# TensorE's order of work by strips of an adjacency matrix: runs of four chunks, one accumulator bank, and the feature store on ACT's queue

## The chip, the cores and the metric

The kernel runs on one core of a Trainium2 chip. The core has engines that work side by side: TensorE (PE in the profile; PEld are its weight loads), VectorE (DVE), ScalarE (ACT), GpSimd (POOL) and SyncE (SP, which here only issues DMA). Each executes its own instructions in order and they meet through semaphores. The metric is the device time of one launch in microseconds; lower is better.

## The reference, cut to what matters

A layer of a graph network on 8192 nodes with 64 features, with a dense 8192 x 8192 float32 adjacency matrix A (268 MB), and a graph attention layer behind it:

```python
h = relu(layernorm(x))                                   # 8192 x 64
hid = tanh(concat([h, t]) @ W1 + b1)
XB = h @ B.T
x = x + hid @ W2 + b2 + A @ XB - A.sum(axis=1, keepdims=True) * XB
h = relu(layernorm(x))
feats = (h @ W).reshape(-1, 8, 8)
scores = leaky_relu(a_self(feats)[i] + a_neigh(feats)[j], 0.2) + (-1e10 * (1 - A))
x = x + relu(softmax(scores, over j) @ feats + bias)
```

The mask is scaled by 1e10, so with these inputs only the largest entry of a row keeps weight in the softmax: the kernel finds the column of each row's largest entry while it reads A once, and fetches the features of that node. A general path for other data stands behind a flag and isn't run with these inputs.

## The kernel before

**Tiling.** A is read once, laid out as 16 strips of 512 rows (`S`), each as 8 chunks (`NC`) of 2 MB: a chunk is 128 partitions by 8 blocks of 512 float32. Chunks go through a ring of four slots in SBUF (`ring`, `RING` 4). SP issues the load of chunk c into its slot when TensorE has counted the old chunk in that slot as done (`pe_chunk`) and so has DVE (`hi_done`), lines 264 to 268.

**TensorE** does two things with each chunk. `products(c)` (L726): 8 matmuls of 128 x 64 weights (h of the nodes) by 512 columns, added into a bank `acc`, two side by side in halves of the bank. `sums(c)` (L734): 8 matmuls of a 128 x 32 block of ones by the same columns into the bank `row_sums`, four side by side. The profile counts two instructions for each of these float32 matmuls, so that one chunk is a row x16 and two chunks x32. A function `chunk` alternates the order so that like stands by like: even chunks products first, odd chunks sums first. A strip in this order is P0 S0 | turns | S1 P1 P2 S2 S3 P3 P4 S4 | turn of h1 | S5 P5 | features, hidden | P6 S6 S7 P7, and P7 stands beside P0 of the next strip. `acc` has two banks, one for even, one for odd strips.

**The small work of a strip** belongs to the strip before: `turn_maxima(s-1)` and `turn_sums(s-1)` (L782, L768 to L775) bring row maxima, sums and products of strip s-1 to node order, `turn_h1(s-1)` (L789) turns the normalised features, `features(s-1)` (L796) multiplies them by the attention layer's weights, and `mlp_hidden(s)` (L754) computes the input of tanh for strip s.

**ACT**, per strip and in this order (`finish_strip(s)`, then `tanh(s+1)`): copy of `acc` (L421) and of `row_sums` (L422) when all 8 chunks are done, copy of the turned sums (L424), the strip of h for the next hidden layer (L415), a square root for the layernorm (L428, with a table load of its own), relu of the turned h1 (L431), copy of the features to SBUF (L433), and the tanh of the next strip (L409, also with a table load). TensorE waits for the copy of the row sums (`rows_copied`) before the first sums of the next strip overwrite their bank; these stand behind the products of chunk 0 (L747). `turn_sums` waits for both copies and for the tanh.

**DVE** folds each chunk into running maxima of 128 x 2048 (L508 to L514), folds these further at the strip's end (L520 to L525), then searches the maxima's places and does the layernorm of strip s-1 between the chunks of strip s. **POOL** fetches candidates, and after the last strip the features of each node's partner, 64 gathers (L367). **SP** stores the features of strip s-1 to DRAM (L275) behind the loads of strip s; it first waits for ACT's copy (`feat_done`), and the loads of the next strip are queued behind that wait.

The loops: ACT and TensorE go over pairs of strips, since the bank alternates; DVE and SP over single ones.

Of the kernel before, what the change touches and what calls it, by code (L numbers as in the profile page):

```python
# [29 lines left out]
D = 64  # L30
# [3 lines left out]
W = 512  # L34
S = N // W
# [16 lines left out]
def build(nc, x, adj, adj_t, w1, w1_t, b1, t_in, w2, b2, b_t, w_gat, w_gat_t, att_self, att_neigh, bias, out):  # L52
    with ExitStack() as ctx:
# [98 lines left out]
        pro_h = sem("pro_h")  # L152
        chunk_in = [sem(f"chunk_in{r}") for r in range(RING)]
        pe_chunk = sem("pe_chunk")
        lo_done = sem("lo_done")
        hi_done = sem("hi_done")
        fold = sem("fold")
# [81 lines left out]
        @block.sync  # L239
        def _(sp):  # L240
            for k, (b0, b1_) in enumerate(((0, 2 * CB), (2 * CB, NB))):
                sp.dma_start(x_pb[:, b0:b1_, :], x_by_p[:, b0:b1_, :]).then_inc(x_in[k], 16)
            for n in range(RING):
                sp.dma_start(slot(n), adj_t[n]).then_inc(chunk_in[n % RING], 16)
            sp.dma_start(x_tq[:, :, :].rearrange("q (s k) d -> q s (k d)", k=TB), x_by_q).then_inc(x_tq_in, 16)

            def load_weights():
                for dst, src in ((w_gat_t_sb[:, :], w_gat_t), (w1_sb[0:D, 0:HID], w1), (w1_sb[D:P, HID:2 * HID], w1), (w2_sb[:, :], w2),
                                 (hid_bias[:, 0:1], b1), (hid_bias[:, 1:2], w1_t),
                                 (hid_bias[:, 2:3], t_in.to_broadcast([HID, 1])),  # L250
                                 (b_t_twice[0:D, :], b_t), (b_t_twice[D:P, :], b_t),
                                 (b_t_diag[0:D, 0:D], b_t), (b_t_diag[D:P, D:2 * D], b_t),
                                 (b2_row[:, :], b2.to_broadcast([P, D])),
                                 (w_ext[0:D, 0:D], w_gat), (w_ext[D:P, FA:FA + D], w_gat), (bias_row[:, :], bias.to_broadcast([P, D]))):
                    sp.dma_start(dst, src).then_inc(consts_in, 16)  # L255
                sp.dma_start(att_col[:, 0:1], att_self).then_inc(att_in, 16)
                sp.dma_start(att_col[:, 1:2], att_neigh).then_inc(att_in, 16)

            sp.wait_ge(pool_const, 12)
            load_weights()  # L260

            def load(s, c):

                sp.wait_ge(pe_chunk, s * NC + (c - RING + 1))
                sp.wait_ge(hi_done, s * NC + (c - RING + 1))
                sp.sem_inc(sp_past, 1)
                src = adj_t[bass.ds(s * NC + c, 1)].rearrange("a p f -> (a p) f")
                sp.dma_start(slot(c), src).then_inc(chunk_in[c % RING], 16)

            def store_feats(s):  # L270

                sp.wait_ge(feat_done, s + 1)
                sp.sem_inc(sp_past, 1)
                dst = feats_by_q[:, bass.ds(s, 1), :].rearrange("q a (k d) -> q (a k) d", d=D)
                sp.dma_start(dst, feats_v[:, bass.ds(s * TB, TB), 0:D]).then_inc(feat_stored, 16)  # L275

            for c in range(RING, NC):
                load(0, c)
            with sp.Fori(1, S) as s:
                for c in range(NC):  # L280
                    load(s, c)
                store_feats(s - 1)
            store_feats(S - 1)
            for g in range(QG):
                sp.wait_ge(out_done, g + 1)
                ts = slice(g * OG, (g + 1) * OG)
                sp.dma_start(out_by_q[:, g * OG // TB:(g + 1) * OG // TB, :],
                             gathered[:, ts, :].rearrange("q (s k) d -> q s (k d)", k=TB)).then_inc(stored, 16)
            sp.wait_ge(stored, 16 * QG)

            sp.wait_ge(flag_done, 1)
            general = sp.value_load(flag[0:1, 0:1], min_val=0, max_val=1)
            with sp.If(general != 0):
                sp.wait_ge(gen_copied, NB // 4)
                sp.dma_start(neigh_dram, h_t[0:HEADS, :]).then_inc(gen_neigh_stored, 16)
                sp.wait_ge(gen_neigh_stored, 16)
                adj_rows = adj.rearrange("(s q k) j -> s k q j", q=P, k=TB)
                out_rows = out.rearrange("(s q k) d -> s k q d", q=P, k=TB)
                with sp.Fori(0, S) as s:
                    for k in range(TB):  # L300
                        ib = s * TB + k
                        sp.wait_ge(gen_head, s * (TB * HEADS) + (k * HEADS + 1))
                        sp.sem_inc(sp_past, 1)
                        sp.dma_start(ring[:, 0:N], adj_rows[bass.ds(s, 1), k].rearrange("a q j -> (a q) j"))\
                            .then_inc(gen_row_in, 16)
                        with sp.Fori(0, HEADS) as h:
                            sp.wait_ge(gen_head, ib * HEADS + h + 1)
                            sp.sem_inc(sp_past, 1)
                            sp.dma_start(ring[:, N:2 * N], neigh_dram[bass.ds(h, 1), :].to_broadcast([P, N]))\
                                .then_inc(gen_neigh_in, 16)  # L310
                        sp.wait_ge(gen_out, s * TB + (k + 1))
                        sp.sem_inc(sp_past, 1)
                        sp.dma_start(out_rows[bass.ds(s, 1), k].rearrange("a q d -> (a q) d"), tmp[:, 0, :])\
                            .then_inc(gen_stored, 16)
                        sp.wait_ge(gen_stored, s * (16 * TB) + (k * 16 + 16))
                        sp.sem_inc(sp_past, 1)
# [57 lines left out]
        def _(act):  # L374
# [40 lines left out]
                    act.copy(h_strip[k * D:(k + 1) * D, :].rearrange("d (m q) -> d m q", q=P),  # L415
                             h_by_k[:, 2 * k:2 * k + 2, bass.ds(s * P, P)]).then_inc(strip_h_done, 1)

            def finish_strip(s, parity, last=False):

                act.wait_ge(pe_chunk, s * NC + NC)  # L420
                act.copy(acc_sb[:, :], acc[parity][:, :]).then_inc(acc_copied, 1)  # L421
                act.copy(row_sb[:, :], row_sums[:, :]).then_inc(rows_copied, 1)  # L422
                act.wait_ge(acc_turned, s + 1)
                act.copy(acc_tq[:, :, :], ps_acc[:, :, 0:D + 1]).then_inc(acc_tq_done, 1)  # L424
                if not last:
# [6 lines left out]
                act.wait_ge(feat_ready, s + 1)  # L432
                act.copy(feats[:, bass.ds(s * (TB * FA), TB * FA)],  # L433
                         ps_feat[:, :, :].rearrange("q t f -> q (t f)")).then_inc(feat_done, 1)

            act.wait_ge(pro_h, 2 * NC)
            strip_h(0)
            act.wait_ge(dve_const, 4)
            tanh(0)
            with act.Fori(0, S // 2 - 1) as r:  # L440
                for k in range(2):
                    finish_strip(2 * r + k, k)
                    tanh(2 * r + k + 1)
            finish_strip(S - 2, 0)
            tanh(S - 1)
            finish_strip(S - 1, 1, last=True)

            act.wait_ge(flag_done, 1)
            general = act.value_load(flag[0:1, 0:1], min_val=0, max_val=1)
# [260 lines left out]
        def _(pe):  # L710
# [6 lines left out]
                    last = pe.transpose(pro_banks[k // 4][:, k % 4, :], x_pb[:, g * CB + k, :], ident[:, :])  # L717
                last.then_inc(pro_turned, 1)

            def products(s, c, parity):  # L720


                pe.wait_ge(chunk_in[c % RING], s * (16 * NC // RING) + 16 * (c // RING + 1))
                for b in range(CB):
                    at = (b % 2) * D
                    last = pe.matmul(acc[parity][at:at + D, :], x_pb[:, c * CB + b, :], slot(c)[:, b * W:(b + 1) * W],  # L726
                                     start=(c == 0 and b < 2), stop=(c == NC - 1 and b >= CB - 2))
                return last

            def sums(c):  # L730
# [3 lines left out]
                    last = pe.matmul(row_sums[at:at + QUAD, :], ones_cols[:, :], slot(c)[:, b * W:(b + 1) * W],  # L734
                                     start=(c == 0 and b < 4), stop=(c == NC - 1 and b >= CB - 4))
                return last

            def chunk(s, c, parity, first=False):


                if c % 2:
                    pe.wait_ge(chunk_in[c % RING], s * (16 * NC // RING) + 16 * (c // RING + 1))
                    sums(c)
                last = products(s, c, parity)
                if c % 2 == 0:
                    if c == 0 and not first:
                        pe.wait_ge(rows_copied, s)  # L747
                    last = sums(c)
                last.then_inc(pe_chunk, 1)

            def mlp_hidden(s):
                pe.wait_ge(strip_h_done, 2 * s + 2)
# [44 lines left out]
                                     h1_t[:, m * P:(m + 1) * P], w_ext[:, :], start=True, stop=True)  # L797
                last.then_inc(feat_ready, 1)

            def strip(s, parity):  # L800

                for c in range(NC):
                    if c == 1:
                        turn_maxima(s - 1)
                        turn_sums(s - 1)
                    chunk(s, c, parity)
                    if c == 4:
                        turn_h1(s - 1, ps_turn)
                    if c == 5:
                        features(s - 1)  # L810
                        mlp_hidden(s)

            for c in range(NC):
                pe.wait_ge(pro_norm, c + 1)
                chunk(0, c, 0, first=True)
                if c == 0:
                    pe.wait_ge(pool_const, 12)
                turn_first(c)
# [6 lines left out]
            pe.wait_ge(dve_const, 6)  # L825
            pe.wait_ge(w_ext_done, 2)
            mlp_hidden(0)
            with pe.Fori(0, S // 2 - 1) as r:
                strip(2 * r + 1, 1)
                strip(2 * r + 2, 0)  # L830
            strip(S - 1, 1)
            turn_maxima(S - 1)
            turn_sums(S - 1)
            turn_h1(S - 1, ps_hid)
# [76 lines left out]
```

## Time and profile before

| | |
|---|---|
| time, median of 3 runs | 904.38 us (903.35 to 905.34) |
| profiled execution, its own time | 904.73 us |
| its span, first to last instruction | 903.5 us |
| mean granted TensorE clock | 0.941 |
| busy: PE, DVE, POOL, ACT | 776.9, 729.3, 173.4, 128.5 us |
| HBM read | 277.10 MB |

All times in the profile are microseconds unless marked ns. A row of the grouped view names line, engine and operation, what is written from what, shapes, count, then busy time, the mean of one, and the idle time ahead with what ended it. In a timeline the first two numbers are the start of a group, from the start of the span, and its length; x is the count, and brackets hold the idle time before it. Matmuls are pipelined, and a group's length includes the tail of its last one, so the start of the next group is the better edge. A granted clock of 1.00 is 2.4 GHz and 0.50 is 1.2 GHz.

The span has three stages: to about 80 us the first strip, together with the layernorm of x; to about 800 us fifteen strips; and the rest, the gathers on POOL, in which TensorE has almost no work.

### The profile page before, as it was taken

The numbers are of one execution on the slowest core, as the hardware profiler recorded it, in microseconds if no ns is written. First come the engines' busy times: TensorE is split into PE (matmuls) and PEld (weight loads), VectorE is DVE, ScalarE is ACT, GpSimd is POOL, SyncE is SP. The second block draws the span as 40 slices with busy tenths as digits, with TensorE's granted clock in tenths as the row PEclk, the third lists the DMA queues.
The fourth block names the chain that finished last, engine by engine and source line by source line (L and its number), as shares of the span: only waits on it lengthen the run. The fifth ranks groups of instructions, "written<-read, shape, count | busy, mean of one in ns | idle before, by whom it ended". The sixth has DMA issues, their size and how long they took to land.

```text
span 903.5 us, 13331 instructions
## 1 busy us (share of the span) xinstructions
PE 776.9 (86%) x5222; PEld 266.7 (30%) x5222; DVE 729.3 (81%) x958; ACT 128.5 (14%) x212; POOL 173.4 (19%) x160
## 2 busy tenths in 40 slices
PE   3898999999999999999999999999999999940000
PEld 1333232333333333333332323233333333320000
DVE  5889968989898989898989898998989897952111
ACT  2424011111111111111010201111111111110000
POOL 1000302020110202020202020202011020217774
PEclk9999999999999999999999999999999999985555
DMA  9797879697979797979798897979797979502221
GB/s 375 280 428 288 321 291 422 271 424 288 425 288 426 284 429 280 429 291 418 319 390 364 345 410 300 420 290 422 289 421 287 425 283 429 214 11 40 60 49 41
DMA packets 37267, 281.58 MB, mean 312 GB/s; under 512 B 14336, under 2 KB 18560, under 8 KB 20736
## 3 DMA queue, kind: packets, MB, share of 16 engines
q1 hardware_dynamic: 33152, 277.12, 74.9%
q0 software_dynamic: 4096, 4.20, 2.0%
q8 instruction: 13, 0.21, 0.1%
q14 instruction: 6, 0.05, 0.0%
HBM read 277.10 MB, written 4.19 MB: 311 GB/s over the span
## 4 chain that ended last, share of the span: by engine, by line
PE 74%; POOL 7%; DVE 5%; issue 4%; DMA 4%; SPq 4%; ACT 0%; POOLq 0%; DVEq 0%
PE acc L726 44%; PE row_sums L734 22%; POOL gathered L367 7%; DMA ring<-in_adj_t 4%; SPq L255 4%; DVE max_hi L514 2%; PE ps_hid L754 2%; PE ps_feat L796 1%; PE ps_xb L775 1%; PE ps_acc L768 1%; PE ps_turn L782 1%; PE ps_acc L771 1%; PE ps_acc L773 1%; PE ps_turn L789 1%; DVE max_lo L513 0%
## 5 line engine op out<-in xcount | busy, mean ns | idle before, releaser
L726 PE MATMUL acc<-ring,x_pb 128*64 128x512 f32 x2048 | 462.8, 601 | 18.4 <-DMA ring<-in_adj_t 18.4
L513 DVE TENSOR_TENSOR max_lo<-max_lo,ring 128x2048 f32<-128x2048 f32 x96 | 220.6, 2298 | 44.7 <-DMA ring<-in_adj_t 44.2
L734 PE MATMUL row_sums<-ring,ones_cols 128*32 128x512 f32 x2048 | 240.0, 597 | 0.0
L726 PEld LDWEIGHTS acc<-ring,x_pb 128*64 128x64 f32 x2048 | 141.0, 138 | 326.1 <-issue 326.1
L514 DVE TENSOR_TENSOR max_hi<-max_hi,ring 128x2048 f32<-128x2048 f32 x96 | 219.7, 2289 | 0.0
L358 POOL DMA_INDIRECT cand<-in_adj,cls_row x64 | 78.0, 1218 | 663.5 <-DVE cls_row L543 648.9
L734 PEld LDWEIGHTS row_sums<-ring,ones_cols 128*32 128x32 f32 x2048 | 56.5, 109 | 151.6 <-issue 149.8
L367 POOL DMA_INDIRECT gathered<-feats_dram,best x64 | 62.8, 981 | 19.5 <-issue 19.5
L651 DVE TENSOR_TENSOR gathered<-gathered,bias_row 128x512 f32<-128x512 f32 x8 | 5.6, 703 | 67.5 <-DMA gathered<-feats_dram,best 67.5
L508 DVE TENSOR_TENSOR max_lo<-ring 128x2048 f32<-128x2048 f32 x16 | 36.7, 2292 | 4.4 <-DMA ring<-in_adj_t 2.5
L510 DVE TENSOR_TENSOR max_hi<-ring 128x2048 f32<-128x2048 f32 x16 | 36.6, 2288 | 4.2 <-DMA ring<-in_adj_t 3.9
L520 DVE TENSOR_TENSOR max_lo<-max_lo,max_hi 128x2048 f32<-128x2048 f32 x16 | 36.7, 2292 | 2.0
L349 POOL TENSOR_TENSOR x_tq<-x_tq,b_row 128x256 f32 x16 | 30.2, 1888 | 37.0 <-DMA bias_row<-in_bias 36.8
L428 ACT ACTIVATE stat<-stat,eps 128x4 f32<-128x4 f32 x16 | 4.8, 298 | 196.0 <-DVE stat L585 196.0
L421 ACT COPY acc_sb<-acc 128x512 f32<-128x512 f32 x16 | 9.4, 586 | 136.6 <-PE acc L726 136.6
L424 ACT COPY acc_tq<-ps_acc 128x260 f32<-128x260 f32 x16 | 6.0, 376 | 106.7 <-PE ps_xb L775 106.7
L409 ACT ACT_TABLE_LOAD x16 | 20.5, 1283 | 2.5 <-PE ps_hid L754 2.3
L428 ACT ACT_TABLE_LOAD x16 | 20.5, 1283 | 0.3
L522 DVE TENSOR_TENSOR max_lo<-max_lo 128x1024 f32<-128x1024 f32 x16 | 19.6, 1225 | 0.5
L754 PE MATMUL ps_hid<-h_strip,w_sb 128*128 128x256 f32 x64 | 17.4, 397 | 3.0 <-ACT h_strip L415 3.0
L433 ACT COPY feats<-ps_feat 128x320 f32 (+1 forms) x16 | 6.8, 426 | 89.6 <-PE ps_feat L796 89.6
L431 ACT ACTIVATE h_t<-ps_turn 128x256 f32<-128x256 f32 x15 | 5.8, 386 | 93.2 <-PE ps_turn L789 93.2
(95 smaller groups left out, 423.3 us busy)
## 6 DMA issues: line engine op xcount, KB each, us to landing
ring<-in_adj_t SPq DMA_DIRECT2D x128, 2048.0 KB, 11.3
x_tq<-in_x SPq DMA_DIRECT2D x1, 2048.0 KB, 30.8
feats_dram<-feats SPq DMA_DIRECT2D x16, 128.0 KB, 2.3
out<-gathered SPq DMA_DIRECT2D x8, 256.0 KB
x_pb<-in_x SPq DMA_DIRECT2D x1, 1536.0 KB, 7.8
cand<-in_adj,cls_row POOLq DMA_INDIRECT x64
gathered<-feats_dram,best POOLq DMA_INDIRECT x64
x_pb<-in_x SPq DMA_DIRECT2D x1, 512.0 KB, 4.6
```

The lines of the kernel that those rows point to most:

```text
L255: sp.dma_start(dst, src).then_inc(consts_in, 16)
L349: pool.tensor_tensor(x1, x1, b2_row[:, :].unsqueeze(1).to_broadcast([P, TB, D]), ALU.add).then_inc(x_b2_done, 1)
L358: pool.indirect_dma_start(out=cand[:, k, :], out_offset=None, in_=classes, in_offset=bass.IndirectOffsetOnAxis(ap=cls_row[:, k:k + 1], axi ...
L367: pool.indirect_dma_start(out=gathered[:, t, :], out_offset=None, in_=feats_dram, in_offset=bass.IndirectOffsetOnAxis(ap=best[:, t:t + 1], ...
L508: dve.tensor_tensor(max_lo[:, :], lo, hi, ALU.max).then_inc(hi_done, 1)
L510: dve.tensor_tensor(max_hi[:, :], lo, hi, ALU.max).then_inc(hi_done, 1)
L513: dve.tensor_tensor(max_lo[:, :], max_lo[:, :], lo, ALU.max).then_inc(lo_done, 1)
L514: dve.tensor_tensor(max_hi[:, :], max_hi[:, :], hi, ALU.max).then_inc(hi_done, 1)
L520: dve.tensor_tensor(max_lo[:, :], max_lo[:, :], max_hi[:, :], ALU.max).then_inc(fold, 1)
L726: last = pe.matmul(acc[parity][at:at + D, :], x_pb[:, c * CB + b, :], slot(c)[:, b * W:(b + 1) * W], start=(c == 0 and b < 2), stop=(c == ...
L734: last = pe.matmul(row_sums[at:at + QUAD, :], ones_cols[:, :], slot(c)[:, b * W:(b + 1) * W], start=(c == 0 and b < 4), stop=(c == NC - 1 ...
L754: last = pe.matmul(ps_hid[:, k * (W // 2):(k + 1) * (W // 2)], w1_sb[:, k * HID:(k + 1) * HID], h_strip[:, :], start=True, stop=True)
```

## The change

TensorE's strip is written out. Its order is S0 S1 | turns | P0 P1 P2 P3 S2 S3 S4 S5 | turn of h1 | P4 P5 P6 P7 S6 S7 | features, hidden, and S0 S1 of the next strip follow. The wait for `rows_copied` stands at the head of the strip. One bank `acc[0]` serves all strips, a new semaphore `acc_full` counts the end of P7, and ACT waits for that before it copies `acc`. Chunks are counted as done behind P0, P1, S2, S3, P4, P5, S6, S7. In the first strip sums stand before products but for chunk 7. ACT issues the store of the features itself, right after its copy of them and a wait for it; SP's stores and their waits are gone. The loops go over single strips.

```diff
         pe_chunk = sem("pe_chunk")
+        acc_full = sem("acc_full")
...
                 src = adj_t[bass.ds(s * NC + c, 1)].rearrange("a p f -> (a p) f")
                 sp.dma_start(slot(c), src).then_inc(chunk_in[c % RING], 16)
 
-            def store_feats(s):
-
-                sp.wait_ge(feat_done, s + 1)
-                sp.sem_inc(sp_past, 1)
-                dst = feats_by_q[:, bass.ds(s, 1), :].rearrange("q a (k d) -> q (a k) d", d=D)
-                sp.dma_start(dst, feats_v[:, bass.ds(s * TB, TB), 0:D]).then_inc(feat_stored, 16)
-
             for c in range(RING, NC):
                 load(0, c)
             with sp.Fori(1, S) as s:
                 for c in range(NC):
                     load(s, c)
-                store_feats(s - 1)
-            store_feats(S - 1)
...
-            def finish_strip(s, parity, last=False):
-
+            def finish_strip(s, last=False):
+
+                act.wait_ge(acc_full, s + 1)
+                act.copy(acc_sb[:, :], acc[0][:, :]).then_inc(acc_copied, 1)
                 act.wait_ge(pe_chunk, s * NC + NC)
-                act.copy(acc_sb[:, :], acc[parity][:, :]).then_inc(acc_copied, 1)
                 act.copy(row_sb[:, :], row_sums[:, :]).then_inc(rows_copied, 1)
                 act.wait_ge(acc_turned, s + 1)
                 act.copy(acc_tq[:, :, :], ps_acc[:, :, 0:D + 1]).then_inc(acc_tq_done, 1)
                 act.wait_ge(feat_ready, s + 1)
                 act.copy(feats[:, bass.ds(s * (TB * FA), TB * FA)],
                          ps_feat[:, :, :].rearrange("q t f -> q (t f)")).then_inc(feat_done, 1)
+                act.wait_ge(feat_done, s + 1)
+                dst = feats_by_q[:, bass.ds(s, 1), :].rearrange("q a (k d) -> q (a k) d", d=D)
+                act.dma_start(dst, feats_v[:, bass.ds(s * TB, TB), 0:D]).then_inc(feat_stored, 16)
 
             tanh(0)
-            with act.Fori(0, S // 2 - 1) as r:
-                for k in range(2):
-                    finish_strip(2 * r + k, k)
-                    tanh(2 * r + k + 1)
-            finish_strip(S - 2, 0)
-            tanh(S - 1)
-            finish_strip(S - 1, 1, last=True)
+            with act.Fori(0, S - 1) as s:
+                finish_strip(s)
+                tanh(s + 1)
+            finish_strip(S - 1, last=True)
...
-            def products(s, c, parity):
-
-
+            def arrived(s, c):
                 pe.wait_ge(chunk_in[c % RING], s * (16 * NC // RING) + 16 * (c // RING + 1))
+
+            def products(c):
+
                 for b in range(CB):
                     at = (b % 2) * D
-                    last = pe.matmul(acc[parity][at:at + D, :], x_pb[:, c * CB + b, :], slot(c)[:, b * W:(b + 1) * W],
+                    last = pe.matmul(acc[0][at:at + D, :], x_pb[:, c * CB + b, :], slot(c)[:, b * W:(b + 1) * W],
                                      start=(c == 0 and b < 2), stop=(c == NC - 1 and b >= CB - 2))
                 return last
...
-
-            def chunk(s, c, parity, first=False):
-
-
-                if c % 2:
-                    pe.wait_ge(chunk_in[c % RING], s * (16 * NC // RING) + 16 * (c // RING + 1))
-                    sums(c)
-                last = products(s, c, parity)
-                if c % 2 == 0:
-                    if c == 0 and not first:
-                        pe.wait_ge(rows_copied, s)
-                    last = sums(c)
-                last.then_inc(pe_chunk, 1)
...
-            def strip(s, parity):
-
-                for c in range(NC):
-                    if c == 1:
-                        turn_maxima(s - 1)
-                        turn_sums(s - 1)
-                    chunk(s, c, parity)
-                    if c == 4:
-                        turn_h1(s - 1, ps_turn)
-                    if c == 5:
-                        features(s - 1)
-                        mlp_hidden(s)
-
+            def strip(s):
+
+                pe.wait_ge(rows_copied, s)
+                for c in (0, 1):
+                    arrived(s, c)
+                    sums(c)
+                turn_maxima(s - 1)
+                turn_sums(s - 1)
+                for c in (0, 1):
+                    products(c).then_inc(pe_chunk, 1)
+                for c in (2, 3):
+                    arrived(s, c)
+                    products(c)
+                for c in (2, 3):
+                    sums(c).then_inc(pe_chunk, 1)
+                for c in (4, 5):
+                    arrived(s, c)
+                    sums(c)
+                turn_h1(s - 1, ps_turn)
+                for c in (4, 5):
+                    products(c).then_inc(pe_chunk, 1)
+                for c in (6, 7):
+                    arrived(s, c)
+                    last = products(c)
+                last.then_inc(acc_full, 1)
+                for c in (6, 7):
+                    sums(c).then_inc(pe_chunk, 1)
+                features(s - 1)
+                mlp_hidden(s)
+
+            pe.wait_ge(pool_const, 3)
             for c in range(NC):
+                arrived(0, c)
+                if c < NC - 1:
+                    sums(c)
                 pe.wait_ge(pro_norm, c + 1)
-                chunk(0, c, 0, first=True)
+                last = products(c)
+                if c == NC - 1:
+                    last.then_inc(acc_full, 1)
+                    last = sums(c)
+                last.then_inc(pe_chunk, 1)
                 if c == 0:
                     pe.wait_ge(pool_const, 12)
...
             pe.wait_ge(w_ext_done, 2)
             mlp_hidden(0)
-            with pe.Fori(0, S // 2 - 1) as r:
-                strip(2 * r + 1, 1)
-                strip(2 * r + 2, 0)
-            strip(S - 1, 1)
+            with pe.Fori(1, S) as s:
+                strip(s)
             turn_maxima(S - 1)
```

## Rows read from the trace of the kernel before

**Rows 1.** page: chain by line; a costliest group (busy, mean ns, idle before).

```profile
PE acc L726 44%; PE row_sums L734 22%; POOL gathered L367 7%; DMA ring<-in_adj_t 4%; SPq L255 4%; DVE max_hi L514 2%; PE ps_hid L754 2%; PE ps_feat L796 1%; PE ps_xb L775 1%; PE ps_acc L768 1%; PE ps_turn L782 1%; PE ps_acc L771 1%; PE ps_acc L773 1%; PE ps_turn L789 1%; DVE max_lo L513 0%
...
L726 PE MATMUL acc<-ring,x_pb 128*64 128x512 f32 x2048 | 462.8, 601 | 18.4 <-DMA ring<-in_adj_t 18.4
```

**Rows 2.** stage of full strips: us, busy by engine, clock, DMA, GB/s.

```profile
166.00:400.00 234.00, 234.00 (x1596) 78.91 (x1594) 212.55 (x275) 31.63 (x54) 33.79 (x25) 1.00 0.88 364
```

**Rows 3.** waits of SP's queue: us in total, times, longest.

```profile
SPq L273 <- ACT feats L433: 198.5, 16, 22.2
```

**Rows 4.** PE timeline, one strip: start, us, line, operation, count, idle.

```profile
403.32 3.65 PE L726 MATMUL acc<-ring,x_pb 128*64 128x512 f32 x16
406.90 3.64 PE L734 MATMUL row_sums<-ring,ones_cols 128*32 128x512 f32 x32
410.47 7.09 PE L726 MATMUL acc<-ring,x_pb 128*64 128x512 f32 x32
417.49 1.92 PE L734 MATMUL row_sums<-ring,ones_cols 128*32 128x512 f32 x16
419.34 0.66 PE L782 MATMUL ps_turn<-ident,runmax 128*128 128x128 f32 x4
...
422.12 1.92 PE L734 MATMUL row_sums<-ring,ones_cols 128*32 128x512 f32 x16
...
449.24 0.81 PE L796 MATMUL ps_feat<-w_ext,h_t 128*128 128x160 f32 x4
...
450.84 3.65 PE L726 MATMUL acc<-ring,x_pb 128*64 128x512 f32 x16
```

**Rows 5.** timeline of ACT behind one strip's features.

```profile
450.17 0.43 ACT L433 COPY feats<-ps_feat 128x320 f32 x1 [5.88 <-PE ps_feat L796]
450.62 1.28 ACT L409 ACT_TABLE_LOAD   x1
```

**Rows 6.** timeline of PE behind two early gaps.

```profile
46.78 5.25 PE L726 MATMUL acc<-ring,x_pb 128*64 128x512 f32 x16 [4.28 <-DMA ring<-in_adj_t]
...
77.37 2.04 PE L754 MATMUL ps_hid<-h_strip,w_sb 128*128 128x256 f32 x4 [2.97 <-ACT h_strip L415]
79.34 4.33 PE L726 MATMUL acc<-ring,x_pb 128*64 128x512 f32 x16
```

**Rows 7.** timeline of ACT, tanh and copies of strip 0.

```profile
79.50 1.28 ACT L409 ACT_TABLE_LOAD   x1 [2.27 <-PE ps_hid L754]
...
81.84 0.60 ACT L422 COPY row_sb<-row_sums 128x512 f32<-128x512 f32 x1
```

**Rows 8.** timeline of SP, store of one strip's features.

```profile
450.99 0.61 SPq L275 DMA_DIRECT2D feats_dram<-feats  x1
```

**Rows 9.** timeline of PE at the end of the last strip.

```profile
791.74 3.65 PE L726 MATMUL acc<-ring,x_pb 128*64 128x512 f32 x16
...
797.32 0.69 PE L768 MATMUL ps_acc<-fold_rows,row_sb 128*64 128x64 f32 x16
...
804.65 0.66 PE L789 MATMUL ps_hid<-ident,h 128*128 128x128 f32 x2 [5.07 <-DVE h L591]
```

**Rows 10.** granted clock in three short stretches (columns as in rows 2).

```profile
46.50:46.75 0.25, 0.00 (x0) 0.00 (x0) 0.25 (x1) 0.00 (x0) 0.00 (x0) 0.74 1.22 524
77.25:77.50 0.25, 0.13 (x1) 0.16 (x1) 0.25 (x1) 0.00 (x0) 0.00 (x0) 0.68 1.02 393
804.00:804.50 0.50, 0.00 (x0) 0.00 (x0) 0.47 (x3) 0.00 (x0) 0.00 (x0) 0.88 0.00 0
```

**Rows 11.** timeline of SP, loads behind a pause.

```profile
119.02 33.43 SPq L268 DMA_DIRECT2D ring<-in_adj_t  x8
```

**Rows 12.** timeline of DVE, arrivals of two chunks.

```profile
126.59 2.29 DVE L508 TENSOR_TENSOR max_lo<-ring 128x2048 f32<-128x2048 f32 x1 [2.51 <-DMA ring<-in_adj_t]
131.49 2.29 DVE L510 TENSOR_TENSOR max_hi<-ring 128x2048 f32<-128x2048 f32 x1 [2.60 <-DMA ring<-in_adj_t]
```

**Rows 13.** DMA issues (page): operation, count, KB each, median us to landing.

```profile
ring<-in_adj_t SPq DMA_DIRECT2D x128, 2048.0 KB, 11.3
```

## The prediction

> **What bounds the kernel now.** I read four views in this order. First the chain of waits by line: the products (L726) are 44% and the row sums (L734) 22% of it, both on TensorE; DMA and DVE have small shares [rows 1]. The grouped lines then say what TensorE waits for: before all 2048 product instructions together it sat idle 18.4 us, for two arrivals of adjacency chunks [rows 1]. The stage between 166 and 400 us settles it: PE is busy 234.00 of 234 us at a granted clock of 1.00, DVE 212.55 [rows 2]. So a strip's period is TensorE's own time, and whatever lengthens it, or makes TensorE wait, is paid in full. SP's long wait for the stored features (198.5 us over 16 strips [rows 3]) costs nothing today, since PE does not starve behind it; to remove it alone earns nothing.
>
> The timeline of one strip shows the period: products of chunks 7 and 0 lie across the strip's edge, and the same row comes back at 450.84 after 403.32, so 47.52 us [rows 4].
>
> **Part 1: fewer changes between products and row sums.** From start to start, products of one chunk (x16) take 3.58 us and of two chunks (x32) 7.02; row sums of one chunk 1.85 and of two 3.57 [rows 4]. Joining two runs thus saves 0.14 (products) or 0.13 (sums), and the marginal chunk costs 3.44 or 1.72. Before, a strip has three product runs of two chunks and two of one (28.22 us), two sum runs of two and four of one (14.54 us): 42.76. The rest, 4.76, is the turns of maxima and sums (2.78, from 419.34 to 422.12), features and hidden layer (1.60, from 449.24 to 450.84) and the turn of h1 (0.38, what is left). After, the order is S01, turns, P0123, S2345 with the h1 turn behind it, P4567, S67, features, hidden: products 2 x (7.02 + 2 x 3.44) = 27.80; sums 2 x 3.57 + 7.01 = 14.15. That is 41.95, or 46.71 with the rest: 0.81 us less per strip, 12.2 us over 15 strips. A run of four is not in the trace. If joining past two brought nothing, 0.28 for the products and 0.13 for the sums would be lost and 0.40 per strip (6.0 us) is left; that it costs something is excluded, as the clock stands at 1.00 through a stage without a pause [rows 2]. I take 12.2, the straight line through both rows.
>
> **Part 2: a new wait at the head of each strip.** This is the large term. The new strip(s) begins with the wait for rows_copied(s), because its first work is row sums. Before, that wait stood behind the products of chunk 0, 3.58 us later. Who brings rows_copied? ACT, which works in order: copy of the features, tanh, copy of acc, copy of row sums. Tanh waits for the hidden layer, and the diff moves features and hidden layer from behind chunk 5 to the very end of the strip, after S67. Thus the copies of acc and row sums, though acc is full long before, queue behind a tanh whose input is TensorE's last work, and TensorE has nothing else to do. Before, ACT did tanh beside chunks 6 and 7.
>
> Length of the gap, counted from the start of the features: their copy on ACT starts 0.93 later and ends at 1.36 (449.24 to 450.17, plus 0.43); the table load for tanh starts at once, 450.62 [rows 4, 5]. From the start of such a load to the end of the copy of row sums, with nothing else in the queue, ACT took 79.50 to 81.84 plus 0.60, that is 2.94 us: this is the tanh of strip 0, the one place where the old kernel runs this very sequence without a pause [rows 7]. Handing over takes about 0.1 (hidden matmuls end at 79.41, load starts at 79.50 [rows 6, 7]). In between lies the feature store, which ACT now issues itself after waiting for its own copy. On SP the issue starts 0.39 after the copy ended (450.60 to 450.99) and takes 0.61, together 1.00 us [rows 5, 8]. An issue on ACT is not in the trace. Its ends are 0 (the queue runs on beside compute) and 1.00 (the same work in the same order); below nothing it can't be, for nothing of ACT's goes. I take 1.00, the only row of the same transfer. Then TensorE may start at 1.36 + 1.00 + 2.94 + 0.10 = 5.40, has 1.60 of own work in that time, and stands still 3.80 us (2.80 with a free issue).
>
> This falls before strips 2 to 15: 14 x 3.80 = 53.2. Before strip 1 there is no feature copy: from 79.34, where products went on, to 82.44 + 0.10, so 3.2 [rows 6, 7]. At the end the last turns of sums need the same copies: they start 5.40 after the last run instead of 1.99 after it (791.74 + 3.58 to 797.32 [rows 9]), and 1.60 of the 5.40 is already counted in the strip: +1.8. What follows on DVE and POOL is unchanged.
>
> **Part 3: the clock after a gap.** Three times in the trace the granted clock fell from 2.4 to 1.2 GHz while TensorE stood: about 4.1 us after the last matmul (fall at 46.6), 2.9 us (at 77.3) and 4.8 us (at 804.4, idle since 799.58) [rows 6, 9, 10]. After the first, a product run took 5.25 instead of 3.65; after the second, hidden matmuls 2.04 instead of 1.03 and products 4.33 instead of 3.65: 1.60 and 1.69 us lost. A gap of 3.8 us lies between these cases. The bounds are 0 and 1.65 per gap; I take half, 0.82, for 15 gaps: 12.4.
>
> The Trainium skill has a rule against this part (TensorE: Matmul & The Clock Gate, Why this matters for your kernels): avoid pauses of some microseconds between bursts of matmuls, else the clock goes back to half. The row at 804.4, with 4.8 us before the fall, agrees only in part; by the rule alone all 15 gaps would pay, and the sum would be the clock rival's below. The same source says of ACT (ScalarE: Activation LUTs, What ACT_TABLE_LOAD costs) that a switch of tables takes a drain of 1.38 us beside the 1.283 of the load. In the 2.94 us above, the load alone is 1.28 and the copy of row sums 0.60 [rows 7]; with tanh and the copy of acc, of some 0.6 each, nothing of a drain has room there; by the page each gap would be 1.38 longer, about 984 in all.
>
> **Part 4: one bank, loads, DVE.** One bank costs nothing: products of a strip start behind the turns of sums, which already waited for the copy of acc. Releases of ring slots bunch: with the strip's head at 0, P0 ends at 9.8, P1 13.3, S2 22.0, S3 23.8, P4 31.1, P5 34.5, S6 43.4, S7 45.1. A load issued to an idle queue at 119.02 landed at 126.59, the next 4.9 later [rows 11, 12]. So chunk 4 lands at 17.4 (needed 23.7), 5 at 22.3 (needed 25.5), 6 at 29.6 (needed 34.5), 7 at 34.5 (needed 38.0): the slack is 3 us or more, and no wait comes. DVE needs 47.52 x 212.55 / 234 = 43.2 us of a strip that now lasts over 50, and its maxima are wanted 3.57 us after the head: chunk 7, landed at 34.5, and what DVE has behind it (under 12 us: a search, two operations of 2.3, the fold) is done by about 46, wanted at 50.5 + 3.57 = 54. Hidden, with some 8 us in hand; what goes beyond these would be paid in full.
>
> **Sum**, against the profiled execution's own 904.73 us (span 903.5; median of the runs 904.38, 0.35 lower and ignored): -12.2 + 53.2 + 3.2 + 1.8 + 12.4 = +58.4, so 963.
>
> **Rivals.** *The issue is free on ACT.* Gaps of 2.80 us, 15 x 1.00 less; and at 2.8 us, under the shortest idle before a fall, the clock may stay: 948 with half the losses, 936 with none. For it: issuing is no compute. Against: SP shows 0.61 us for it, and in-order waiting for feat_done comes on top. *The clock falls in every gap:* 15 x 1.65 = 24.8 in place of 12.4, 975; for it stands the fall after 2.9 us, against it the 4.8. *The ring is late:* were each load 11.3 us in flight (the median of all 128 [rows 13]), chunk 5 would land behind chunk 4 at 21.1 + 4.9 = 26.0, 0.5 late, and chunk 7 at 38.2, 0.2 late: 15 x 0.7, so 974; with the clock falling in every gap too, 986. Against: that median includes queueing behind other loads. *The other side, not slower:* a change between products and sums costs much more than the starts show, since matmul ends are modelled and a run of four may stream better. Place: the six runs fewer per strip. It has to outweigh 70.6 us, so 90 changes at 0.78 us each; at 0.80 the time would be 903. Starts are not modelled, and two independent pairs of them say 0.13 and 0.14. That the wait is met early, so that the change is the plain gain of 12 us (892), would need ACT to copy ahead of tanh, which its program order forbids; I count both as one chance.
>
> **Chances.** Forecast (issue holds ACT, some clock losses; its own range 951 to 974) 0.62; free issue 0.20; clock in every gap 0.10; ring late 0.05; not slower 0.03. The range runs from the free issue without clock losses (935) past the clock in every gap (975) into that case with a late ring (982). A difference under 0.2% (1.8 us) can't be told from none here: faster 0.03, same 0.01, slower 0.96.
>
> **What would show it.** In the changed profile the row sums at a strip's head have an idle of 2.8 to 3.9 us ahead of them, 14 times, ended by ACT's copy of row_sb; ACT's idle before the copy of acc is near zero; product runs x64 take 13.9 us; the period is 50 to 52 us; the clock is 0.5 in stretches behind some gaps only. If PE has no idle at the strip's head, part 2 is wrong and with it the forecast; if products x64 take 13.9 but the gap is 2.8, only the issue was mis-sized.

## The result and the profile after

The changed kernel takes 975.58 us (median of four runs, 975.15 to 975.8) against 904.52 us: the ratio is 1.0786 (95% interval 1.0767 to 1.0805), 71 us slower. Its profiled execution has a span of 973.3 us, 69.8 more than before, and a mean granted clock of 0.907 after 0.941.

First the page of the changed kernel: the chain by line, and the two TensorE groups that share the chunks (columns as in [rows 1]).

```profile
PE acc L720 44%; PE row_sums L728 26%; POOL gathered L359 6%; SPq L256 3%; PE ps_feat L777 1%; ACT hidden L401 1%; ACTq L430 1%; PE ps_xb L756 1%; PE ps_acc L749 1%; PE ps_turn L763 1%; ACT row_sb L415 1%; PE ps_acc L752 1%; PE ps_acc L754 1%; DMA ring<-in_adj_t 1%; ACT acc_sb L413 1%
...
L720 PE MATMUL acc<-ring,x_pb 128*64 128x512 f32 x2048 | 448.3, 594 | 0.0
L728 PE MATMUL row_sums<-ring,ones_cols 128*32 128x512 f32 x2048 | 263.3, 664 | 74.0 <-ACT row_sb L415 54.2
```

Lines of ACT have entered the chain, and the idle time that ACT's copy of row sums ends is 54.2 us; before there was none. The mean of one product fell from 601 to 594 ns, but that of a row-sum instruction rose to 664.

The timeline of PE over one strip of the changed kernel shows both (start, length, group, idle ahead):

```profile
396.87 5.03 PE L728 MATMUL row_sums<-ring,ones_cols 128*32 128x512 f32 x32 [3.64 <-ACT row_sb L415]
401.83 0.66 PE L763 MATMUL ps_turn<-ident,runmax 128*128 128x128 f32 x4
...
404.60 13.95 PE L720 MATMUL acc<-ring,x_pb 128*64 128x512 f32 x64
418.49 7.07 PE L728 MATMUL row_sums<-ring,ones_cols 128*32 128x512 f32 x64
425.49 0.44 PE L770 MATMUL ps_turn<-ident,h 128*128 128x128 f32 x2
425.86 13.95 PE L720 MATMUL acc<-ring,x_pb 128*64 128x512 f32 x64
439.75 3.64 PE L728 MATMUL row_sums<-ring,ones_cols 128*32 128x512 f32 x32
443.32 0.81 PE L777 MATMUL ps_feat<-w_ext,h_t 128*128 128x160 f32 x4
443.96 1.03 PE L735 MATMUL ps_hid<-h_strip,w_sb 128*128 128x256 f32 x4
448.62 6.45 PE L728 MATMUL row_sums<-ring,ones_cols 128*32 128x512 f32 x32 [3.63 <-ACT row_sb L415]
```

A run of four chunks of products takes 13.89 us from start to start (404.60 to 418.49), of row sums 7.00: the straight line through [rows 4] to 0.01 us. But this strip's period is 51.75 us in place of 47.52: a gap of 3.63, and the first row sums last 5.03 or 6.45 where the same 32 instructions take 3.64 at the strip's end.

What ACT does in the gap (the changed kernel's ACT timeline, which answers to [rows 5] and [rows 7]; ACTq is its queue issuing the DMA):

```profile
444.25 0.43 ACT L426 COPY feats<-ps_feat 128x320 f32 x1 [17.90 <-PE ps_feat L777]
444.88 0.57 ACTq L430 DMA_DIRECT2D feats_dram<-feats  x1
445.55 1.28 ACT L401 ACT_TABLE_LOAD   x1 [0.87 <-ACT feats L426]
446.84 0.69 ACT L401 ACTIVATE hidden<-ps_hid,hid_bias 128x512 f32<-128x512 f32 x1
447.43 0.58 ACT L413 COPY acc_sb<-acc 128x512 f32<-128x512 f32 x1
447.89 0.60 ACT L415 COPY row_sb<-row_sums 128x512 f32<-128x512 f32 x1
```

ACT waits 17.9 us for the features, then everything comes at once: copy, issue (0.87 of idle on the engine), table load, tanh, both copies; 0.13 us after the last of them TensorE starts.

The granted clock around that same gap (stretch, length, PE, PEld, DVE, ACT and POOL busy, clock, DMA share, GB/s):

```profile
445.00:447.50 2.50, 0.00 (x0) 0.00 (x0) 2.50 (x2) 1.94 (x3) 0.00 (x0) 1.00 0.99 413
447.50:448.50 1.00, 0.00 (x0) 0.00 (x0) 1.00 (x1) 0.99 (x3) 0.00 (x0) 0.50 1.03 442
448.75:454.25 5.50, 5.50 (x28) 1.26 (x31) 4.29 (x2) 0.00 (x0) 0.00 (x0) 0.50 0.96 388
454.50:457.00 2.50, 2.50 (x60) 1.83 (x52) 1.92 (x1) 0.00 (x0) 0.00 (x0) 1.00 0.02 5
```

It fell to 1.2 GHz 2.5 us after the last matmul (444.99) and stayed there until some 5.7 us into the work. Behind the next gap, whose work went on at 501.80, it fell only after TensorE had begun:

```profile
501.80:502.00 0.20, 0.20 (x4) 0.16 (x8) 0.00 (x0) 0.00 (x0) 0.00 (x0) 1.00 0.19 82
502.00:502.25 0.25, 0.25 (x4) 0.00 (x0) 0.00 (x0) 0.00 (x0) 0.00 (x0) 0.74 1.60 668
```

Three neighbouring heads of strips, further on:

```profile
605.63 6.45 PE L728 MATMUL row_sums<-ring,ones_cols 128*32 128x512 f32 x32 [3.63 <-ACT row_sb L415]
...
658.81 5.34 PE L728 MATMUL row_sums<-ring,ones_cols 128*32 128x512 f32 x32 [3.63 <-ACT row_sb L415]
...
710.88 5.04 PE L728 MATMUL row_sums<-ring,ones_cols 128*32 128x512 f32 x32 [3.64 <-ACT row_sb L415]
```

Against 3.64 these are losses of 2.81, 1.70 and 1.40 us, and the three values come round every three strips (the first three heads measure 1.39, 2.73 and 1.70). All 15 together lose 29.4 us.

The account of the 69.8 us (15 gaps of 54.2 us in all, of which 3.17 ahead of strip 1): gaps at strips 2 to 15, 54.2 - 3.17 = 51.05; clock 29.4; the head of strip 1 stands 3.5 later (82.84 for 79.34); what follows the matmuls of the last strip (from 795.32 before, 864.09 after) is 1.0 longer; 15 strips of TensorE's own work are 700.9 in place of 713.1, -12.2; and two waits for h1 (2.17) and the slow products of strip 1 (0.68) of the old kernel are gone, -2.9. The sum is 69.8, to the rounding of its terms.

The 1.0 at the end hides more. The last turns of sums wait too:

```profile
867.81 1.12 PE L749 MATMUL ps_acc<-fold_rows,row_sb 128*64 128x64 f32 x16 [3.12 <-ACT row_sb L415]
```

They start 3.72 us after that edge in place of 2.00. The clock fell in this gap as well (0.50 from 868 to 870 us), which is most of the 1.3 us by which TensorE then takes longer to the turn of h1. From POOL's first fetch of the last strip on, where the program is the same, the new run is 2.0 us shorter; why isn't known.

### The profile page after: what moved, and what is told of

It is laid out like the page before. It is cut to its first block, busy times and chain, and to the rows that moved or that the text cites. A ratio compares the mean times of both kernels' runs of the same rounds, so it can differ in the third digit from the quotient of the medians.

```text
span 973.3 us, 13367 instructions
## 1 busy us (share of the span) xinstructions
PE 793.6 (82%) x5222; PEld 281.2 (29%) x5222; DVE 727.3 (75%) x958; ACT 126.8 (13%) x212; POOL 140.1 (14%) x160
## 4 chain that ended last, share of the span: by engine, by line
PE 77%; POOL 7%; issue 5%; ACT 4%; SPq 4%; ACTq 1%; DMA 1%; DVE 1%; POOLq 0%; DVEq 0%
PE acc L720 44%; PE row_sums L728 26%; POOL gathered L359 6%; SPq L256 3%; PE ps_feat L777 1%; ACT hidden L401 1%; ACTq L430 1%; PE ps_xb L756 1%; PE ps_acc L749 1%; PE ps_turn L763 1%; ACT row_sb L415 1%; PE ps_acc L752 1%; PE ps_acc L754 1%; DMA ring<-in_adj_t 1%; ACT acc_sb L413 1%
## 5 line engine op out<-in xcount | busy, mean ns | idle before, releaser
L720 PE MATMUL acc<-ring,x_pb 128*64 128x512 f32 x2048 | 448.3, 594 | 0.0
L728 PE MATMUL row_sums<-ring,ones_cols 128*32 128x512 f32 x2048 | 263.3, 664 | 74.0 <-ACT row_sb L415 54.2
L720 PEld LDWEIGHTS acc<-ring,x_pb 128*64 128x64 f32 x2048 | 144.1, 137 | 282.6 <-issue 280.8
L350 POOL DMA_INDIRECT cand<-in_adj,cls_row x64 | 61.1, 954 | 768.0 <-DVE cls_row L536 753.3
L728 PEld LDWEIGHTS row_sums<-ring,ones_cols 128*32 128x32 f32 x2048 | 67.0, 120 | 252.4 <-issue 246.6
L401 ACT ACT_TABLE_LOAD x16 | 20.5, 1283 | 14.9 <-ACT feats L426 12.2
L341 POOL TENSOR_TENSOR x_tq<-x_tq,b_row 128x256 f32 x16 | 14.0, 872 | 37.5 <-DMA bias_row<-in_bias 37.2
L531 DVE FIND_INDEX8 idx_cls<-top_cls,ps_turn 128x8 uint32<-128x128 f32 x64 | 17.4, 291 | 0.3 <-issue 0.3
## 6 DMA issues: line engine op xcount, KB each, us to landing
feats_dram<-feats ACTq DMA_DIRECT2D x16, 128.0 KB, 10.3
```

Of the source, the lines that this page charges most:

```text
L350: pool.indirect_dma_start(out=cand[:, k, :], out_offset=None, in_=classes, in_offset=bass.IndirectOffsetOnAxis(ap=cls_row[:, k:k + 1], axi ...
L401: act.activation(hidden[:, :], ps_hid[:, :], ACT.Tanh, bias=hid_bias[:, 3:4])\
L720: last = pe.matmul(acc[0][at:at + D, :], x_pb[:, c * CB + b, :], slot(c)[:, b * W:(b + 1) * W], start=(c == 0 and b < 2), stop=(c == NC - ...
```

## The experiments

The theory: TensorE's new wait is ACT's program order, in which the copy of row sums stands behind a tanh fed by TensorE's last work; a part of the loss is the gap itself, the other the clock behind it. All kernels were timed against the kernel before on the same chip (903.39 us for half of the filler, both repairs together and the store moved alone; 904.71 for the other four).

**Filler in the gap.**

```diff
                 features(s - 1)
                 mlp_hidden(s)
+                for b in range(CB):
+                    at = (b % 2) * D
+                    pe.matmul(acc[1][at:at + D, :], x_pb[:, b, :],
+                              x_pb[:, 0:CB, :].rearrange("p b d -> p (b d)"), start=(b < 2), stop=(b >= CB - 2))
```

> The changed kernel, with eight matmuls of the products' size added behind the hidden layer of each strip, into the unused second bank (their result is read by nobody). They last about 3.44 us and so fit in the 3.63 us in which TensorE waits for the copy of row sums. Theory (the loss is a pure gap of 3.63 us per strip plus a clock loss of 1.96 us per strip, 29.4 us in all): the wait shrinks to about 0.2 us, the strip still begins at the same moment, the clock stays at 1.00 and the row sums at the head take 3.57 again: 975.6 - 29, about 946. Rival (the slow first row sums are not the clock's but come from the bank or from DMA traffic): the head stays slow, 974 to 976. Rival (the filler does not fit and delays the strip): above 976.

Measured: 948.00 us, ratio 1.0478 (1.046 to 1.0495). Its PE timeline:

```profile
433.19 3.65 PE L812 MATMUL acc<-x_pb 128*64 128x512 f32 x16
436.89 3.64 PE L728 MATMUL row_sums<-ring,ones_cols 128*32 128x512 f32 x32
```

More work, 27.6 us less time: the head takes 3.64 again. Only the first gap, ahead of the loop and without filler, keeps its loss; from 130 to 845 us the granted clock is 1.00. The clock's part is thus shown apart from the gap: some 28 of the 71 us.

**Half of the filler**, against the kernel with all of it:

```diff
-                for b in range(CB):
+                for b in range(4):
...
-                              x_pb[:, 0:CB, :].rearrange("p b d -> p (b d)"), start=(b < 2), stop=(b >= CB - 2))
+                              x_pb[:, 0:CB, :].rearrange("p b d -> p (b d)"), start=(b < 2), stop=(b >= 2))
```

> The changed kernel with four filler matmuls behind the hidden layer in place of eight (their result is read by nobody): TensorE then stands still for about 1.9 us per strip in place of 3.63, at unchanged starts of the strips. Theory (the clock falls when TensorE has stood for long enough, and the shortest idle before a fall seen so far is 2.8 us): no fall, 948 us as with the full filler. Rival (any gap of this kind costs the clock): losses as in the changed kernel, 970 to 976; losses in a part of the gaps lie between, about 2 us each.

Measured: 946.74 us, ratio 1.0479 (1.0462 to 1.0497), the same as with the full filler.

```profile
437.19 3.64 PE L728 MATMUL row_sums<-ring,ones_cols 128*32 128x512 f32 x32 [1.77 <-ACT row_sb L415]
```

All 14 heads with an idle of 1.76 to 1.93 us take 3.64, and the clock is again 1.00 from 130 to 845 us: a gap of this size costs its own length and no more.

**Store back on SP**, behind the fourth load of the strip after next:

```diff
-                act.wait_ge(feat_done, s + 1)
-                act.dma_start(dst, feats_v[:, bass.ds(s * TB, TB), 0:D]).then_inc(feat_stored, 16)
...
+            with sp.Fori(2, S) as s:
+                for c in range(RING):
+                    load(s, c)
+                store_feats(s - 2)
+                for c in range(RING, NC):
+                    load(s, c)
```

> The changed kernel, with the store of the features back on SP's queue (of strip s-2, behind the first four loads of strip s, where it is long ready). Theory (the issue on ACT lies in the chain with 0.87 us): gap of 2.76 instead of 3.63, 14 times, 12 us less; if the clock loss stays the same per gap, 963; if gaps of 2.8 us keep the clock in part, down to 940. Rival (the issue runs on beside ACT's next work and costs nothing): gap and time as in the changed kernel, 975.6.

Measured: 959.20 us, ratio 1.0598 (1.058 to 1.0616). Heads of two strips in its PE timeline, and the table load in ACT's:

```profile
440.73 5.33 PE L738 MATMUL row_sums<-ring,ones_cols 128*32 128x512 f32 x32 [2.78 <-ACT row_sb L428]
...
491.93 5.33 PE L738 MATMUL row_sums<-ring,ones_cols 128*32 128x512 f32 x32 [2.78 <-ACT row_sb L428]
```

```profile
437.21 0.42 ACT L439 COPY feats<-ps_feat 128x320 f32 x1 [17.90 <-PE ps_feat L787]
437.65 1.28 ACT L414 ACT_TABLE_LOAD   x1
```

The gap is 0.85 shorter: the issue had stood between copy and table load. That is 12 us; the other 4 are the clock, which now loses 1.6 to 1.7 behind each of the 15 gaps in place of 1.96 on average. The first of these gaps is 3.17 long, the other 14 are 2.78: one of 2.78 us still costs the clock every time.

**Features and hidden layer earlier:**

```diff
                 last.then_inc(acc_full, 1)
+                features(s - 1)
+                mlp_hidden(s)
                 for c in (6, 7):
                     sums(c).then_inc(pe_chunk, 1)
-                features(s - 1)
-                mlp_hidden(s)
```

> The changed kernel, with features and hidden layer moved ahead of the row sums of chunks 6 and 7. Theory (ACT in program order holds the copy of row sums back behind a tanh whose input comes last): tanh and the copy of acc now lie beside the last row sums; what is left of the gap is the copy of row sums and two hand-overs, 0.7 to 0.8 us; no clock loss. 973.3 (span) - 15 x (3.63 - 0.75) - 29.4 + 0.9, about 902 to 905 us in all, the same as the old kernel. Rival (ACT's work itself, not its order, is the bound): the gap stays above 2 us and the time above 940.

Measured: 904.83 us, ratio 1.0 (0.9991 to 1.001). ACT and PE at a strip's edge:

```profile
414.86 0.58 ACT L413 COPY acc_sb<-acc 128x512 f32<-128x512 f32 x1
416.06 0.59 ACT L415 COPY row_sb<-row_sums 128x512 f32<-128x512 f32 x1 [0.62 <-PE row_sums L728]
```

```profile
416.78 3.64 PE L728 MATMUL row_sums<-ring,ones_cols 128*32 128x512 f32 x32 [0.78 <-ACT row_sb L415]
```

Now ACT waits for TensorE, no longer the other way round. Two moved calls take back all 71 us with not an instruction more or less, which shows the order as the cause. What is left, 0.78 us per strip, eats the gain of the longer runs.

**Two banks for the row sums** (the bank that the change left unused), loops over pairs of strips again:

```diff
-                pe.wait_ge(rows_copied, s)
...
-                    last = pe.matmul(row_sums[at:at + QUAD, :], ones_cols[:, :], slot(c)[:, b * W:(b + 1) * W],
+                    last = pe.matmul((acc[1] if bank else row_sums)[at:at + QUAD, :], ones_cols[:, :], slot(c)[:, b * W:(b + 1) * W],
...
-                act.copy(row_sb[:, :], row_sums[:, :]).then_inc(rows_copied, 1)
+                act.copy(row_sb[:, :], (acc[1] if bank else row_sums)[:, :]).then_inc(rows_copied, 1)
```

> The changed kernel, with the row sums of odd strips in the bank that the change left unused, and without the wait at the strip's head; features and hidden layer stay at the end. Theory: the first row sums need no copy any more; the turns of sums behind them start 1.60 + 3.57 + 0.58 = 5.75 us after the features and ACT is ready 5.2 after them, so no gap, no clock loss, and the 0.81 us per strip of the longer runs is left: 890 to 893 us. Rival (the gain of the runs is not real, or is given back by late loads or by DVE): 900 to 908, with new waits for DMA or DVE.

Measured: 896.26 us, ratio 0.991 (0.9894 to 0.9927); single runs lie between 894.12 and 898.05, wider than any other kernel here.

```profile
405.52 0.81 PE L780 MATMUL ps_feat<-w_ext,h_t 128*128 128x160 f32 x4
406.17 1.03 PE L738 MATMUL ps_hid<-h_strip,w_sb 128*128 128x256 f32 x4
407.13 3.64 PE L731 MATMUL row_sums<-ring,ones_cols 128*32 128x512 f32 x32
```

No gap, and the next head comes at 453.79: a period of 46.66. The profiled run (894.12) is near the theory's 890 to 893, the median is not. In this profile the last turns of sums wait 2.8 us for ACT, and PE waits five times for h1 from DVE (2.7 us in all): a small part of the rival is there. What makes its runs differ stays open.

**Both repairs together**, the two diffs above on one kernel:

```diff
-                pe.wait_ge(rows_copied, s)
...
                 last.then_inc(acc_full, 1)
+                features(s - 1)
+                mlp_hidden(s)
                 for c in (6, 7):
-                    sums(c).then_inc(pe_chunk, 1)
-                features(s - 1)
-                mlp_hidden(s)
+                    sums(c, bank).then_inc(pe_chunk, 1)
```

> The changed kernel with both repairs: features and hidden layer ahead of the row sums of chunks 6 and 7, and two banks for the row sums without the wait at the head, so that the row sums of chunks 6, 7, 0, 1 are one run of four. Theory (TensorE is the bound, joining two runs saves 0.13 us): 0.13 less per strip than the two banks alone, 2 us, and the tail's wait for the copies falls away (2.8 us to some 1): 890 to 894. Rival (at a period of 46.6 us DVE and the loads are the bound, for which the spread of 894 to 898 with two banks speaks): no better than 896, with PE waiting for DVE or DMA in the trace.

Measured: 889.36 us, ratio 0.9832 (0.9814 to 0.985), 14 us faster than the kernel before and the fastest of all here.

```profile
450.76 3.64 PE L731 MATMUL row_sums<-ring,ones_cols 128*32 128x512 f32 x32
454.22 3.62 PE L731 MATMUL acc<-ring,ones_cols 128*32 128x512 f32 x32
457.76 0.66 PE L766 MATMUL ps_turn<-ident,runmax 128*128 128x128 f32 x4
```

The row sums of two strips are one run, 7.00 us in place of twice 3.57, and the tail's wait is gone. TensorE still waits for DVE's h1, three times and 2.75 us in all, so at this period DVE is close to being the bound in some strips.

**The kernel before, with only the store moved to ACT:**

```diff
-                store_feats(s - 1)
-            store_feats(S - 1)
...
+                act.wait_ge(feat_done, s + 1)
+                dst = feats_by_q[:, bass.ds(s, 1), :].rearrange("q a (k d) -> q (a k) d", d=D)
+                act.dma_start(dst, feats_v[:, bass.ds(s * TB, TB), 0:D]).then_inc(feat_stored, 16)
```

> The kernel before, with only the feature store moved from SP's queue to ACT's. Theory (SP's wait of 198.5 us held loads back that nobody missed, and ACT has 5 us or more in hand where the issue of 0.87 us falls): no change, 903.5 to 905.5 us. Rival (earlier loads help DVE and so TensorE's two waits for h1): up to 2 us less. Rival (the issue delays tanh and with it TensorE): 13 us more, 917.

Measured: 900.89 us, ratio 0.9971 (0.9961 to 0.998): 2.5 us faster (1.8 to 3.5 by the interval). The theory, that this earns nothing, falls; its first rival, up to 2 us, is the nearest. PE's turn of h1 and of the last maxima in this kernel:

```profile
774.72 0.44 PE L783 MATMUL ps_turn<-ident,h 128*128 128x128 f32 x2
...
792.87 0.66 PE L776 MATMUL ps_turn<-ident,runmax 128*128 128x128 f32 x4
```

Neither has an idle time ahead; before, the same turn of h1 waited 1.02 us (and an earlier one 1.15) and the maxima 1.34 for DVE; of the last, 0.59 comes back as a wait of the turns of sums for ACT. By [rows 11, 12] DVE had waited for a load issued only after SP's store; that this is what made it late is read from there for the early wait, and not shown for the others.

## Why the prediction came out as it did

The direction and the mechanism were right, and the time, 975.6 for 963, lies in the range. Step by step:

- **What bounds the kernel**: right for TensorE. Wrong in one sentence, that the removal of SP's wait alone earns nothing: moving the store alone brought 2.5 us, and TensorE's waits for DVE in two strips and at the end went with it.
- **Part 1, longer runs**: 12.2 us forecast, 12.2 measured. It is real, and it is what the repaired kernel keeps.
- **Part 2, the wait**: 3.80 us per gap forecast, 3.63 measured; 53.2 for 51.05 over 14. The 1.00 for the issue was 0.87, so the SP row was the right one to take. Strip 1: 3.2 forecast, 3.5 measured. The tail's wait: 1.8 forecast, 1.7 measured, though only 1.0 of it is seen at the end.
- **Part 3, the clock**: the term that was mis-sized, 12.4 us for 29.4, so 17.0 too little. The other terms were 5.6 too high together, half of it from the 2.9 us of old waits and slow products that the sum left out. Of the miss of 12.6 us, 11.4 lie so in the span (69.8 for 58.4), the rest outside it. Two things in the clock's term were off. I took half of the gaps as spared, from three falls that came 2.9, 4.1 and 4.8 us after the last matmul; all 15 paid, and the tail's gap too. And a gap that pays can pay 2.81, not the 1.65 of the two that the old trace held. The flaw in the reading: a fall need not come within the gap. Behind the gap at 498.2 the clock fell at 502.1, after work had gone on at 501.80, so that delays until a fall don't say how long a gap is safe. The Trainium skill (TensorE: Matmul & The Clock Gate, Why this matters for your kernels) says that pauses of some microseconds between bursts of matmuls put the clock back to half. I weighed this at 0.10, and it is what the 15 gaps of 3.17 to 3.81 us show. In the experiments gaps of 1.8 us lost nothing (14 of 14), and gaps of 2.8 us lost the clock like those of 3.6 (14 of 14).
- **The rivals**: the clock in every gap (975) is the case that came. That its figure is met within 1 us is luck: it priced the clock at 24.8 us for 29.4, and the terms that it shared with the forecast were 5.6 too high. Free issue: refuted by 0.87 us of idle and by the run with the store on SP. Late ring: products have no idle ahead in the profile after. The other side fell with the gap.
- **The drain**: the Trainium skill (ScalarE: Activation LUTs, What ACT_TABLE_LOAD costs) gives 1.38 us of it with each switch of tables. It did not appear here: tanh starts 1.29 us after the load starts, in the gap as well.

## What to carry to other kernels

When work moves to the end of a loop body, follow what it feeds through the other engine's program order to the first wait of the next round: an engine that is busy 13% of the time can hold up the bound one if all its work arrives at once. Put the producer of such a chain ahead of a block long enough to cover it, or give the waiting result a second bank. And price a gap of TensorE of about 3 us at half as much again as its length, or more (here 1.96 us on average beside 3.63, and 1.6 to 1.7 beside 2.78).

## What the runs showed of the hardware

- The clock's loss behind a gap depends on more than the gap's length: with 3.63 us it goes 2.81, 1.70, 1.40 from strip to strip, and with 2.78 us it is 1.6 to 1.7 at every strip, whose period was then 51.2 us. What sets the order isn't shown. Matmuls that fill a part of the gap save more than they cost: 3.44 us of filler work per strip, or half of it, brought some 28 us against the changed kernel, by the ratios to the kernel before.
- The 128 KB feature store landed 2.3 us after its issue when SP issued it between loads, and 10.3 us after when ACT issued it beside them (median of 16 in both). The queue alone doesn't decide it: in the two kernels with features ahead of the last row sums it landed in 2.7 and 2.8 us from ACT's queue, with SP's late store in 9.8. Nothing waited for it here.
